# Steps between causal heads moved into the middle of the next batch, and the low-rank products of q and k issued in turn ahead of a value projection

## What is computed

```
x = layernorm(x + L0_attn(x))   # q, k, v = x @ W.T + b; 16 heads of 8; causal softmax(q k / sqrt(8)) v; @ Wo.T + bo
x = layernorm(x + L0_ffn(x))    # 8 experts of 128 -> 256 -> 128, relu, gates of the top 2
x = layernorm(x + L1_attn(x))   # q = (x @ q_a[h]) @ q_b[h], k = (x @ k_a[h]) @ k_b[h], rank 64; 16 causal heads of 8
x = layernorm(x + L1_ffn(x))    # 16 heads of 4, not causal, then 8 experts, gelu, top 2, weighted by 0.3
```

## Time and profile before

| | |
|---|---|
| median of three runs | 1207.62 us |
| the profiled execution, its own time | 1212.2 us |
| its span | 1210.5 us |
| PE busy | 1106.1 us, 91% of the span |
| DVE busy | 868.8 us, 72% |
| ACT busy | 772.7 us, 64% |
| POOL busy | 268.1 us, 22% |

### The profile page before, as it was taken

How to read it: one execution, slowest core, us unless ns; L and a number is a source line. 1 busy time by engine, 2 the same in 40 slices (tenths; PEclk the granted TensorE clock), 3 DMA queues, 4 the chain that set the end, 5 groups by cost and what they waited for, 6 DMA issues and landing times. The chain is left out here.

```text
span 1210.5 us, 24804 instructions
## 1 busy us (share of the span) xinstructions
PE 1106.1 (91%) x8768; PEld 605.3 (50%) x8840; DVE 868.8 (72%) x2061; ACT 772.7 (64%) x1547; POOL 268.1 (22%) x795
## 2 busy tenths in 40 slices
PE   8899998999999989999989998888888898899996
PEld 6566665655766655666655542221112221137774
DVE  4888888683444477888777889899999989904433
ACT  4367666666444426667666657888888778874443
POOL 4234332332002012533233411111110011000001
PEclk8899999999999999999999989999999989999999
DMA  7145431110000701343221311102111000000000
GB/s 192 51 112 138 116 94 31 33 40 3 1 1 15 172 11 38 77 102 97 71 83 33 62 30 32 30 11 36 36 32 31 20 12 16 7 1 1 10 9 18
DMA packets 39546, 57.65 MB, mean 48 GB/s; under 512 B 9392, under 2 KB 14976, under 8 KB 39040
## 3 DMA queue, kind: packets, MB, share of 16 engines
q1 hardware_dynamic: 39424, 56.06, 18.8%
HBM read 30.81 MB, written 24.64 MB: 46 GB/s over the span
## 5 line engine op out<-in xcount | busy, mean ns | idle before, releaser
L875 ACT ACTIVATE probs<-bank 128x512 f32<-128x512 f32 x1088 | 574.4, 601 | 239.0 <-PE bank L1272 237.9
L991 DVE TENSOR_REDUCE tile_max<-bank 128x1 f32<-128x512 f32 (+3 forms) x1152 | 611.6, 592 | 41.7 <-PE bank L1257 36.3
L1257 PE MATMUL bank<-qk 125*128 125x128 bf16 (+2 forms) x1664 | 389.3, 312 | 60.7 <-DVE tile_max L991 46.9
L1272 PE MATMUL bank<-qk 128*128 128x128 bf16 (+4 forms) x1606 | 363.2, 306 | 5.7 <-ACT probs L875 5.3
L1301 PE MATMUL bank<-probs,v_head 128*32 128x512 f32 (+3 forms) x3328 | 305.9, 457 | 0.1
L1257 PEld LDWEIGHTS bank<-qk 125*128 125x128 bf16 (+1 forms) x1664 | 132.8, 97 | 316.5 <-DVE tile_max L991 243.8
L1158 DVE SCALAR_TENSOR_TENSOR acc<-bank,gate,acc 128x128 f32<-128x128 f32 x256 | 72.0, 344 | 156.7 <-PE bank L1427 156.7
L1301 PEld LDWEIGHTS bank<-probs,v_head 128*32 128x32 f32 x3328 | 140.8, 109 | 53.8 <-issue 30.7
L1272 PEld LDWEIGHTS bank<-qk 128*128 128x128 bf16 (+1 forms) x1664 | 133.4, 97 | 58.4 <-ACT probs L875 20.7
L895 ACT ACTIVATE probs<-bank,sb_b 128x512 f32<-128x512 f32 x128 | 81.0, 684 | 117.9 <-PE bank L1416 117.9
L985 DVE TENSOR_REDUCE tile_max<-bank 128x4 f32<-128x512 f32 x128 | 87.3, 687 | 83.3 <-PE bank L1257 82.7
(11 more groups left out here) (133 smaller groups left out, 642.4 us busy)
## 6 DMA issues: line engine op xcount, KB each, us to landing
qk<-qk_parts SPq DMA_DIRECT2D x160, 144.0 KB
qk_parts<-q_parts SPq DMA_DIRECT2D x48, 192.0 KB, 2.4
qk_parts<-k_parts SPq DMA_DIRECT2D x48, 192.0 KB, 3.0
qk_parts<-q_parts SPq DMA_DIRECT2D x24, 96.0 KB, 2.3
qk_parts<-k_parts SPq DMA_DIRECT2D x24, 96.0 KB, 2.9
sb_w<-in_w SPq DMA_DIRECT2D x8, 256.0 KB, 3.9
sb_w<-in_w SPq DMA_DIRECT2D x2, 1024.0 KB, 7.0
qk<-neg_rows SPq DMA_DIRECT2D x96, 6.0 KB
```

The lines of the kernel that those rows point to most:

```text
L875: nc.scalar.activation(probs[:, hd.probs_place(c), :], S2[i % len(S2)][:], ACT.Exp, scale=hd.a.scale).then_inc(sem("probs"), 1)
L991: ins = nc.vector.tensor_reduce(tile_max[:, hd.slot, t, which:which + 1], s1[:, at:at + P * count], AX.X, ALU.max)
L1257: ins = mm(s1[:, at:at + P * count], qk[hd.query_rows, hd.place, 0, P * t:P * (t + 1)], qk[hd.query_rows, hd.place, 1, P * k0:P * (k0 + co ...
L1272: ins = mm(s2[:, at:at + P * count], qk[hd.key_rows, hd.place, 1, P * j:P * (j + 1)], qk[hd.key_rows, hd.place, 0, P * q0:P * (q0 + count) ...
```

## The change

Four edits:

1. `effective_weights` is called in `qkv_first`, between q and k of sequence 1 and v of sequence 1, and its loop has the head outside: a product of q, then one of k, 16 times. The semaphore `eff_ps` becomes `eff_q` and `eff_k`.
2. Five 128 x 128 float32 products of the identity with itself are issued on PE ahead of the first transposes. They write a bank that nothing has used yet.
3. PE does the steps of causal heads where it does those of the other heads: in the next batch, behind its second pair of chunks.
4. ACT and DVE take the steps of causal heads behind the third chunk in place of the second, and `rests` moves from the third to the fourth.

```diff
--- before.py
+++ after.py
@@ -111,13 +111,11 @@
 
         if self.a.causal:
             self.place = g % RING
-            self.read_after = 1
             self.data_rows = [slice(0, 36), slice(64, 100)]
             self.query_rows = slice(0, P // 2 + QUERY_ROWS)
             self.key_rows = slice(0, P)
             self.max_row = P // 2 + QUERY_ROWS
         else:
-            self.read_after = 2
             half = self.n // 2 % 2
             self.place = self.n % 2 + 2 * (self.n // 4 % 2)
             self.data_rows = [slice(64 * half, 64 * half + 36)]
@@ -793,7 +791,7 @@
                     second_first(m + 2)
                     second_first(m + 3)
                 for w in range(2):
-                    act.wait_ge(sem("eff_ps"), w + 1)
+                    act.wait_ge(sem(("eff_q", "eff_k")[w]), 1)
                     nc.scalar.activation(w_eff[w][:], bank[w][:, 0:D], ACT.Copy).then_inc(sem("eff"), 1)
 
             def between(place):
@@ -875,7 +873,7 @@
                         nc.scalar.activation(probs[:, hd.probs_place(c), :], S2[i % len(S2)][:], ACT.Exp,
                                              scale=hd.a.scale).then_inc(sem("probs"), 1)
                         before = at_place_before(run, g, k)
-                        if c == batch[hd.read_after] and before is not None:
+                        if c == batch[2] and before is not None:
                             between(before)
                     if k == 0 and g + 1 < run.stop:
                         rows(g + 1)
@@ -1019,9 +1017,9 @@
                             find_max(i)
                         found = upto
                         before = at_place_before(run, g, k)
-                        if c == batch[hd.read_after] and before is not None:
+                        if c == batch[2] and before is not None:
                             between(before)
-                        if c == batch[hd.read_after + 1] and before is not None:
+                        if c == batch[3] and before is not None:
                             rests(before)
                     if k == 0 and g - 2 >= run.start and HEADS[g - 2].ends_group:
                         normalise(GROUP[g - 2])
@@ -1228,16 +1226,19 @@
                 values_first(0)
                 transposed_upto(1)
                 queries_and_keys(1)
+                effective_weights()
                 values_first(1)
 
             def effective_weights():
 
                 loaded(pe, "low_rank")
-                for w, (a_n, b_n) in enumerate((("q_aT", "q_b"), ("k_aT", "k_b"))):
-                    for h in range(H):
+                for h in range(H):
+
+                    for w, (a_n, b_n) in enumerate((("q_aT", "q_b"), ("k_aT", "k_b"))):
                         ins = mm(bank[w][:, 8 * h:8 * h + 8], w_sb[a_n][:, h, :], w_sb[b_n][:, h, :],
                                  start=True, stop=True)
-                    ins.then_inc(sem("eff_ps"), 1)
+                        if h == H - 1:
+                            ins.then_inc(sem(("eff_q", "eff_k")[w]), 1)
 
             def scores_by_query(i):
                 g, c = query_chunk(i)
@@ -1394,7 +1395,7 @@
                         asked = upto
                         scores_by_key(g, c)
                         before = at_place_before(run, g, k)
-                        if c == batch[1] and before is not None and not HEADS[before[1]].a.causal:
+                        if c == batch[1] and before is not None:
                             between(before)
                     if k == 0 and g + 1 < run.stop:
                         max_rows(g + 1)
@@ -1404,8 +1405,6 @@
                         probs_by_v(g, k - 1)
                     elif g > run.start:
                         probs_by_v(g - 1, len(HEADS[g - 1].a.batches) - 1)
-                    if hd.a.causal:
-                        between(at_head(g, k))
                 return asked
 
             def experts(f, last):
@@ -1440,8 +1439,10 @@
                     between(at_unit(f, m, 1))
 
             pe.wait_ge(sem("identity"), 2)
+
+            for _ in range(5):
+                mm(SUM[:, 0:P], ident[:], ident[:], start=True, stop=True)
             qkv_first()
-            effective_weights()
             pe.wait_ge(sem("eff"), 2)
             pe.wait_ge(sem("constants"), CONSTANTS)
             for f, run in enumerate(RUNS):
```

## The result

The changed kernel takes 1196.12 us in the median of five runs (1194.08 to 1197.0); before it was 1207.62 in as many. The ratio is 0.9897, with a 95% interval of 0.9882 to 0.9912: 1.0% faster. The prediction was 1197.3, in a range from 1188 to 1203.5. The span of the profiled execution is 1194.4 us, 16.1 less than that of before, which had lain 4.6 above its median.

The account below looks back on a forecast made before the run. PE was taken as the bound, busy 91% of the span, with 16.4 us of idle time around steps. Start 5.1 plus steps 5.2 gave 10.3 us off, a median of 1197.3, range 1188 to 1203.5.

Parts of the forecast that it names:

- The start: Work before DVE's first maxima: alternating products, copy wait off the path and warm-up products together gain 5.1 us.
- the steps: Causal heads with steps: moving PE's steps and ACT's and DVE's takings gains 5.2 us, between -4.6 and 16.4.
- Edit 1: Low-rank products and second value projection at the start: 12.65 us becomes 8.5, gain 4.1, plus 0.5 for k's copy.
- the rival with no gain from alternating: Low-rank products: alternating q and k gains nothing, the start is 1.0 us worse, total 1203.4; chance 0.08.
- Edit 2: Five identity products before the first transposes: gain 0.5 us, between -0.3 and +1.5, if the higher clock comes sooner.
- ACT's copy of the maxima: PE's waits at steps, 3.0 and 1.6 us: copy is done two pairs into the next batch; 1.1 kept, gain 3.5.
- DVE's maxima: PE's waits of 3.3 and 2.1 us: DVE has chunks during products and step; 1.2 kept, gain 4.2.
- DVE's remainder: PE's waits for the remainder of q or k, 1.7 + 1.1 us: 0.3 more at each of four, -1.2.
- The hand-over: New waits for bank SHARED at max_rows: 0.30 us at seven steps that ACT takes, -2.1; at bound -7.6.
- The clock: First twelve heads with steps, a 108 us window: at most 2.2 us lost to a clock of 0.98; 0.8 gained back.
- The start alone gains: Rival: the steps' waits only change place, the hand-over eating the gain; total 1202.5 us, chance 0.17.
- The slower case: Rival: PE waits the full 1.08 us at all 15 SHARED hand-overs within a batch; total 1218.7 us, chance 0.06.

Follow-up runs that it names:

- in_a_row: The changed kernel with the low-rank products of all q first, then all k, still ahead of the second value projection: 0.9958 of before, 1202.64 us.
- start_only: The kernel before with only the low-rank products alternating q and k and moved ahead of the second value projection: 0.9955 of before.
- all_but_warm: The changed kernel without the five identity products ahead of the first transposes: 0.992 of before, 1196.92 us.
- mixed: The changed kernel with causal heads' takings one chunk sooner, except what DVE does alone, left behind the third chunk: 0.9854 of before, median 1190.5 us.
- first_pair: The changed kernel with causal heads' steps on PE behind the first pair of chunks and ACT's and DVE's takings behind the second chunk: 0.9882 of before.
- take_early: The changed kernel with ACT's and DVE's takings of causal heads' steps back where they were before: 0.9869 of before, median 1191.92 us.
- warm_only: The kernel before with only the five identity products added ahead of the first transposes: 0.9986 of before.
- late_only: The kernel before with only ACT's and DVE's takings of causal heads' steps one chunk later: 1.0025 of before.
- steps_only: The kernel before with causal heads' steps on PE moved into the next batch and ACT's and DVE's takings one chunk later: 0.9949 of before.

## Why the prediction was right, step by step

**The sign, the size and the split held.** The start was to bring 5.1 us and the steps 5.2. Measured alone, the start's two edits bring 5.4 and 1.7, the steps 6.2, all by their ratios; together it is 12.4 by the ratio and 11.5 by the medians. So both halves gained more than was forecast. Inside the steps two terms missed in opposite directions, by more than their sum did: that 1197.3 lies so near to 1196.12 is in part luck.

**Edit 1** was right in mechanism. Pairs of loads do overlap, 0.11 us from pair to pair, and without the turn the gain is gone (`in_a_row`); so the rival with no gain from alternating is out. (It gave two reasons that are not one: a window that had let the loads overlap already, and loads that wait for the matmuls of their pair.) Its two durations were too long: 4.6 us for the products, which took 3.7, and 3.9 for the value projection, which took 2.05. I let the clock fall as it did before. But products that take a third of the time were over before it fell: the granted clock is 1.00 through the products, the projection and on to 33.4 us. For the projection that is a lucky trace. Of the six traces with the turn, it took 2.05 us in three (the changed kernel, `start_only`, `all_but_warm`) and 2.69, 2.82 and 3.34 in the others (`mixed`, `first_pair`, `take_early`), where the clock fell while it ran. The first maxima came at 24.57 instead of the 28.5 that I gave. Of these 9.1 us against the first trace the ratios of the two parts show 7.1; a single profile of a start that hangs on the clock isn't the median.

**Edit 2**: +0.5 predicted, 1.7 (0 to 3.4) measured alone, and 0.8 to 2.8 within the changed kernel, not told from none. The four projection instructions took 1.98 in five of the six traces with the five products and 3.78 in that of `take_early`.

**Edits 3 and 4, by kind of wait.** ACT's copy of the maxima: I kept 1.1 us of 4.6; it was 5.6, as said above, and keeps 0.3 in each stretch. This term was too small, and the mechanism right: edit 3 alone makes the whole of it. DVE's maxima: 1.2 kept of 5.4 was too hopeful, 2.4 + 0.9 = 3.3 stay, and here the mechanism was wrong. I took the burst of the products with v and the step for the cause, and a step two pairs away from it for the cure; with edit 3 alone these waits are as long as before (table above). What shortened them is edit 4. Why is not shown; behind DVE's statistics and normalising, which end at 189.3 and 191.2, PE still waits 0.36 and 0.66 us in the changed kernel, at 190.02 and 191.89, so these blocks are a likely part of what stays. DVE's remainder: 1.2 worse predicted, 4.0 - 2.8 = 1.2 measured. That is a difference too: edit 3 makes it 1.7 better and edit 4 2.9 worse. The hand-over: 0.30 seven times, 2.1; in the two windows six of 0.4 are there and one of 0.6 at `turn_sums`, 3.0. The clock: 0.8 predicted; 1.6 lie between the twelve heads with its fall (108.1) and without (106.48, `warm_only`). No trace with edit 3 has it, but neither have those of `warm_only` and `late_only`, so it isn't shown that edit 3 prevents it. The windows came to 104.1 and 83.8, where I had written 105.5 and 83.5. By these waits and the clock some 4.7 us of the 5.9 that the two windows gained are accounted for; the rest is not traced.

**The rivals.** "The start alone gains" is out by `steps_only`. The slower case, waits of 1.08 at all 15 places, is out as a size, and right as a direction: edit 4 alone makes the kernel 3 us slower, and waits of 0.4 to 0.7 us of this kind stand in its trace, 3.6 in all, with 1.3 more for the remainder. Shorter waits elsewhere make up for a part of that, so the sum of the kinds is no proof of the 3 us. I had priced edits 3 and 4 as one; that one of them gains some 3 us more than both was in my terms (-1.2 and -2.1), but I drew no forecast from it.

## What to carry to other kernels

Work that passes through a single bank should not stand directly behind another use of that bank whose result is taken late: here two chunks further on, where ACT had made its copy, the waits for it fell from 5.6 us to 0.6. The taking has to follow at once, because the bank's next tenant waits; taking it a chunk later cost 3 us by itself, and 3 us in the two windows on top of edit 3. Two sets of narrow products on different halves of the partitions should alternate one by one, since PE looked only three loads ahead. And edits that belong together should still be undone one at a time: the sum of the two here hid that one of them lost time.

## What was not expected of the hardware

- Narrow products with 64 rows run two at a time with no loss: 29 loads of one kind take 3.31 us, and 32 pairs take 3.7, at the same clock.
- The clock fell during the narrow products in all six traces that have them in a row, and in none of the six with the turn. There they were over in 3.7 us; the clock then fell in the projection behind them in three of the six. Whether the shorter time or the two products at once makes the difference isn't shown.
- With the products in a row, k's first matmul starts before the last three of q, which stand ahead of it in the program: 25.15 against 25.35, 25.57 and 25.78 us in before, 20.83 against 20.94, 21.05 and 21.16 in `in_a_row`.
- Two traces of one kernel, before, differ by 4.9 us in span while their causal heads with steps agree to 0.06 us. Windows between fixed events told apart what whole times could not.
